# Expert layers of a macaron block: up-projection weights as the stationary operand, fed from two fixed buffers per half

## What is computed

```python
x = hidden_states.reshape(-1, H)                       # H = 256
probs = jax.nn.softmax(x @ router_w.T, axis=-1)        # 8 experts
topk_weights, selected_experts = jax.lax.top_k(probs, 2)
for e in range(E):
    ew = jnp.sum(topk_weights * (selected_experts == e), axis=-1, keepdims=True)
    h = x @ w1[e].T                                    # 256 -> 2 * 512
    gate = jax.nn.silu(h[:, :I])                       # I = 512
    y = h[:, I:] * gate @ w2[e].T                      # 512 -> 256
    out = out + y * ew
```

## Time and profile before

| | before |
|---|---|
| median of the runs | 2212.82 us |
| profiled execution, device time | 2211.96 us |
| its span, first to last instruction | 2210.2 us |
| first FFN's slots | about 131 to 552 us |
| second FFN's slots | about 1762 to 2188 us |
| TensorE busy over the span | 1602.6 us (73%) |
| VectorE, ScalarE, GpSimd busy | 1189.6, 632.5, 735.4 us |

### The profile page before, as it was taken

One profiled execution on the slowest core, in us unless ns is written; L12 is line 12 of the kernel. 1 busy time (PEld: TensorE's weight loads), 2 busy tenths in 40 slices (PEclk: granted clock), 3 DMA queues, 4 the chain that ended last, 5 costly groups with the idle time before them and its releaser, 6 DMA issues. The chain is left out here.

```text
span 2210.2 us, 62919 instructions
## 1 busy us (share of the span) xinstructions
PE 1602.6 (73%) x23284; PEld 1062.9 (48%) x23285; DVE 1189.6 (54%) x3478; ACT 632.5 (29%) x1646; POOL 735.4 (33%) x988
## 2 busy tenths in 40 slices
PE   4359999999477278572777536786357299999995
PEld 4336666666135265251643436444355156666663
DVE  7513434444256875559764696667766334344442
ACT  2111111111356234453343633446323111111110
POOL 3722222222044151550514704238044212222221
PEclk9999999999677587775887856886668599999998
DMA  9443223232101000110001000010000272323234
GB/s 293 146 160 48 45 45 45 46 45 39 52 3 28 1 19 20 41 30 0 20 20 40 10 20 15 5 58 9 3 11 29 95 233 45 48 43 48 43 48 100
DMA packets 83844, 113.32 MB, mean 51 GB/s; under 512 B 13048, under 2 KB 74944, under 8 KB 81600
## 3 DMA queue, kind: packets, MB, share of 16 engines
q1 hardware_dynamic: 57120, 75.91, 11.2%
q0 software_dynamic: 26592, 35.67, 9.7%
HBM read 63.65 MB, written 52.08 MB: 52 GB/s over the span
## 5 line engine op out<-in xcount | busy, mean ns | idle before, releaser
L591 PE MATMUL ffn_bank<-ffn_w,ffn_tileT 128*128 x1136 | 539.0, 597 | 7.4 <-DMA ffn_w<-in_w2t_dram 3.9
L712 POOL DMA_INDIRECT x<-ffn_yout,ffn_place x142 | 221.1, 1557 | 651.2 <-DVE ffn_yout L679 587.1
L650 ACT ACTIVATE ffn_gate<-ffn_bank 128x512 f32<-128x512 f32 x142 | 84.8, 597 | 706.2 <-PE ffn_bank L591 706.2
L607 PE MATMUL ffn_bank<-ffn_w,ffn_actT 128*128 x1136 | 268.6, 379 | 1.8 <-DVE ffn_actT L693 1.8
L591 PEld LDWEIGHTS ffn_bank<-ffn_w,ffn_tileT 128*128 128x128 f32 x1136 | 195.5, 192 | 148.7 <-issue 148.5
L607 PEld LDWEIGHTS ffn_bank<-ffn_w,ffn_actT 128*128 128x128 f32 x1136 | 215.7, 190 | 91.2 <-issue 69.2
L693 DVE COPY ffn_actT<-ffn_bank 128x512 f32<-128x512 f32 x142 | 98.1, 691 | 170.8 <-PE ffn_bank L599 170.8
L685 DVE TENSOR_TENSOR ffn_gate<-ffn_gate,ffn_bank 128x512 f32<-128x512 f32 x142 | 97.6, 687 | 167.1 <-PE ffn_bank L591 167.1
L1444 PE MATMUL at_bank<-pass_right,pass_left 32*32 32x48 f32 x3072 | 52.2, 231 | 83.0 <-DVE pass_right L1316 63.5
L580 PE MATMUL ffn_bank<-ffn_ident,ffn_tile 128*128 128x128 f32 x284 | 55.6, 278 | 77.5 <-DMA ffn_tile<-xs 77.3
L599 PEld LDWEIGHTS ffn_bank<-ffn_ident,ffn_gate 128*128 128x128 f32 x568 | 71.2, 141 | 73.9 <-issue 73.7
(11 more groups left out here) (493 smaller groups left out, 3252.1 us busy)
## 6 DMA issues: line engine op xcount, KB each, us to landing
ffn_tile<-xs SPq DMA_DIRECT2D x142, 130.0 KB, 2.1
ffn_w<-in_w1t_dram SPq DMA_DIRECT2D x16, 1024.0 KB, 5.2
ffn_w<-in_w2t_dram SPq DMA_DIRECT2D x16, 512.0 KB, 6.2
ffn_x<-in_x_dram SPq DMA_DIRECT2D x16, 256.0 KB, 4.8
x<-ffn_x SPq DMA_DIRECT2D x16, 256.0 KB, 6.1
pass_xa<-x SPq DMA_DIRECT2D x12, 256.0 KB, 3.6
pass_xr<-x SPq DMA_DIRECT2D x12, 256.0 KB, 2.7
x<-pass_xr SPq DMA_DIRECT2D x12, 256.0 KB, 2.1
```

The costliest lines, as they stand in the source:

```text
L591: t = pe.matmul(bank[:, :], rowsT[b][:, k * P:(k + 1) * P], w1[:, bass.ds(e * 2048 + (k * 1024 + half * INNER), INNER)], start=(k == 0), s ...
L607: t = pe.matmul(p_y[b], actT[b][:, k * P:(k + 1) * P], w2[:, bass.ds(e * 1024 + k * DIM, DIM)], start=(k == 0), stop=(k == ICH - 1))
L650: act.activation(gate[b][:, :], p_g[b][:, :], ACT.Silu).then_inc(s_silu, 1)
L712: pool.indirect_dma_start(total, bass.IndirectOffsetOnAxis(ap=place[b][:, 0:1], axis=0), yout[b][:, :], None, compute_op=ALU.add).then_inc ...
```

## The change

The stationary and the moving operand of the up-projection change places. For each slot, half and 128-column chunk of the half, a 128x128 block of `w1` is now loaded as the stationary operand and the 128 turned tokens move past. The product comes out with the inner dimension on partitions, which is the layout that `down` wants, so `turn_act` and the copy to `actT` are gone and `inner` takes the place of both `gate` and `actT`. The stationary blocks are not read at a register's address: `fetch` copies the slot's half of `w1` (128 x 1024 f32) to a fixed buffer, half 0 on ScalarE behind Silu of the slot before, half 1 on VectorE behind the product of the slot before. Each copy reads the expert's number into a register and waits for that expert's weights.

```diff
+    half_now = [[sb(f"{n}{i}", [P, KCH, INNER]) for i in range(2)] for n in ("gate_now", "up_now")]
+    def fetch(eng, copy, m, b, half):
+        e = eng.value_load(table.expert[0:1, bass.ds(m, 1)], min_val=0, max_val=EXPERTS - 1)
+        eng.wait_ge(wts.s, e * 32 + 32)
+        src = w1[:, :].rearrange("p (e k s f) -> p e k s f", e=EXPERTS, k=KCH, s=2)[:, bass.ds(e, 1), :, half, :]
+        copy(half_now[half][b][:, :, :], src.rearrange("p e k f -> p (e k) f")).then_inc(s_now[half], 1)
 # TensorE
-            def up(m, b, e, half):
+            def up(m, b, half):
+                pe.wait_ge(s_now[half], m + 1)
                 if half == 0:
-                    pe.wait_ge(wts.s, e * 32 + 32)
                     pe.wait_ge(s_xTs, m + 1)
                     if not early(m):
-                        pe.wait_ge(s_aTs, m - 1)
+                        pe.wait_ge(s_act, m - 1)
                 bank = (p_g if half == 0 else p_u)[b]
-                for k in range(KCH):
-                    t = pe.matmul(bank[:, :], rowsT[b][:, k * P:(k + 1) * P],
-                                  w1[:, bass.ds(e * 2048 + (k * 1024 + half * INNER), INNER)],
-                                  start=(k == 0), stop=(k == KCH - 1))
+                for i in range(ICH):
+                    for k in range(KCH):
+                        t = pe.matmul(bank[:, i * P:(i + 1) * P],
+                                      half_now[half][b][:, k, i * P:(i + 1) * P],
+                                      rowsT[b][:, k * P:(k + 1) * P], start=(k == 0), stop=(k == KCH - 1))
-            def turn_act(m, b):
+            def down(m, b, e):
                 pe.wait_ge(s_act, m + 1)
-                for k in range(ICH):
-                    t = pe.transpose(p_t[b][:, k * P:(k + 1) * P], gate[b][:, k * P:(k + 1) * P], ident[:, :])
-                t.then_inc(s_aT, 1)
-            def down(m, b, e):
-                pe.wait_ge(s_aTs, m + 1)
...
-                e = expert(m)
-                up(m, b, e, 0)
-                if not lead:
-                    turn_act(m - 1, 1 - b)
-                up(m, b, e, 1)
+                up(m, b, 0)
+                up(m, b, 1)
                 if not lead:
                     down(m - 1, 1 - b, expert(m - 1))
 # ScalarE
-                act.activation(gate[b][:, :], p_g[b][:, :], ACT.Silu).then_inc(s_silu, 1)
+                act.activation(inner[b][:, :], p_g[b][:, :], ACT.Silu).then_inc(s_silu, 1)
+                if not last:
+                    fetch(act, act.copy, m + 1, 1 - b, 0)
 # VectorE
-                dve.tensor_tensor(gate[b][:, :], gate[b][:, :], p_u[b][:, :], ALU.mult).then_inc(s_act, 1)
+                dve.tensor_tensor(inner[b][:, :], inner[b][:, :], p_u[b][:, :], ALU.mult).then_inc(s_act, 1)
+                if not last:
+                    fetch(dve, dve.tensor_copy, m + 1, 1 - b, 1)
                 if not (isinstance(m, int) and m == 0):
                     weigh(m - 1, j if b == 1 else j - 1, 1 - b)
                 if not last:
                     meta(m + 1, j + (b == 1), 1 - b)
-                dve.wait_ge(s_aT, m + 1)
-                if not early(m):
-                    dve.wait_ge(s_y, m - 1)
-                dve.tensor_copy(actT[b][:, :], p_t[b][:, :]).then_inc(s_aTs, 1)
```

More of the change, by code:

```diff
@@ L522, in experts @@
     rowsT = [sb(f"tileT{i}", [P, KCH * P]) for i in range(2)]
-    gate = [sb(f"gate{i}", [P, INNER]) for i in range(2)]
-    actT = [sb(f"actT{i}", [P, ICH * P]) for i in range(2)]
+    inner = [sb(f"inner{i}", [P, ICH * P]) for i in range(2)]
     yout = [sb(f"yout{i}", [P, DIM]) for i in range(2)]
@@ L529, in experts @@
     w1, w2 = wts.w1, wts.w2
+    half_now = [[sb(f"{n}{i}", [P, KCH, INNER]) for i in range(2)] for n in ("gate_now", "up_now")]
     p_x = [psum[0][:, 0:DIM], psum[1][:, 0:DIM]]
     p_g, p_u = [psum[2], psum[3]], [psum[4], psum[5]]
-    p_t = p_g
     p_y = [psum[6][:, 0:DIM], psum[7][:, 0:DIM]]
@@ L536, in experts @@
     s_g, s_u, s_silu, s_act = sem("g"), sem("u"), sem("silu"), sem("act")
-    s_aT, s_aTs, s_y, s_ys, s_go, s_id = sem("aT"), sem("aTs"), sem("y"), sem("ys"), sem("go"), sem("id")
+    s_now = [sem("gate_now"), sem("up_now")]
+    s_y, s_ys, s_go, s_id = sem("y"), sem("ys"), sem("go"), sem("id")
     def early(m):
         return isinstance(m, int) and m < 2
+    def fetch(eng, copy, m, b, half):
[3 more added lines that the diff above has]
+        copy(half_now[half][b][:, :, :], src.rearrange("p e k f -> p (e k) f")).then_inc(s_now[half], 1)
     with nc.Block() as block:
@@ L606, in down @@
                 for k in range(ICH):
-                    t = pe.matmul(p_y[b], actT[b][:, k * P:(k + 1) * P],
+                    t = pe.matmul(p_y[b], inner[b][:, k * P:(k + 1) * P],
                                   w2[:, bass.ds(e * 1024 + k * DIM, DIM)],
@@ L636, in _ @@
             step(PAIRS, 0, last=True)
-            turn_act(SLOTS - 1, 0)
             down(SLOTS - 1, 0, expert(SLOTS - 1))
@@ L641, in _, with step @@
         def _(act):
-            def step(m, b):
+            def step(m, b, last=False):
                 act.wait_ge(s_xT, m + 1)
@@ L648, in step @@
                 if not early(m):
-                    act.wait_ge(s_aT, m - 1)
-                act.activation(gate[b][:, :], p_g[b][:, :], ACT.Silu).then_inc(s_silu, 1)
+                    act.wait_ge(s_y, m - 1)
+                act.activation(inner[b][:, :], p_g[b][:, :], ACT.Silu).then_inc(s_silu, 1)
+                if not last:
+                    fetch(act, act.copy, m + 1, 1 - b, 0)
+            fetch(act, act.copy, 0, 0, 0)
             for b in range(2):
@@ L655, in _ @@
                     step(2 * j + b, b)
-            step(SLOTS - 1, 0)
+            step(SLOTS - 1, 0, last=True)
         @block.vector
@@ L689, in step @@
                     meta(m + 1, j + (b == 1), 1 - b)
-                dve.wait_ge(s_aT, m + 1)
-                if not early(m):
-                    dve.wait_ge(s_y, m - 1)
-                dve.tensor_copy(actT[b][:, :], p_t[b][:, :]).then_inc(s_aTs, 1)
+            fetch(dve, dve.tensor_copy, 0, 0, 1)
             meta(0, 0, 0)
```

## The result

The changed kernel took 2173.9 us, the median of four runs (2167.7 to 2186.2), beside 2212.2 us (2205.8 to 2214.2, four runs, one more than in the section on the kernel before): a ratio of 0.984, with a 95% interval of 0.981 to 0.987. The forecast was 2169 with a range of 2151 to 2225. The profiled execution took 2178.0 us, its span 2176.1.

What follows compares the result with a forecast made beforehand. TensorE's own work was taken to set the FFN slot: 5.83 to 5.50 us, 133 x 0.33 = 43.9 less, 1.2 more at the second FFN's start, so 42.7 off 2212.0 gives 2169.3, stated as 2169; range 2151 to 2225.

Steps and rivals of the forecast that it cites:

- The price of a pair: Up-projection on TensorE: load and 128-column matmul run side by side, 0.111 us a pair, 3.55 for 32; break-even 0.121.
- The rival in which a load shows: Up-projection: load and matmul don't hide each other wholly, 0.163 us a pair, slot 7.17, time 2390; chance 0.15.
- the 8 columns: Routing matmuls' moving columns: 0.014 us at 1.2 GHz if loads waited for matmuls; the 0.214 pace was said to exclude it.
- The slot: TensorE's steady FFN period: 0.22 turning rows, 3.55 up-projection, 1.73 down-projection, together 5.50 us, 0.33 less than 5.83.
- The start of the second FFN: A copy of 1.04 us now lies between the first weights' landing and the first matmul: some 1.2 us more.
- Late tiles as before: Some 7 slots early in the second FFN, with tiles late behind weight DMAs, were taken as unchanged.
- The copies: Weight copies of 128x1024, 1.04 us on ScalarE and 0.69 on VectorE, hidden beside TensorE's work with 0.7 to spare.
- the tile ring: VectorE's copy, `weigh`, `meta`, SyncE's load, DMA: hidden by 0.7 us, 0.15 with longer copy; late-tile rival 2205, chance 0.12.
- TensorE needs the copied half itself only after the next half 0, at 7.3.: Deadline of VectorE's copy of half 1's weights, counted in us from the start of half 0 of slot m.
- Registers on TensorE: One of two register reads per slot goes, costing nothing while TensorE's queue is full; up to 0.74 us gained behind late tiles.
- The scatter as the bound: Rival: VectorE's copy and GpSimd's descriptor work block each other, scatter's ring 5.80 us, no gain, 2209; chance 0.04.
- the change doesn't do what it says: Rival: half 0 finds its block missing, ScalarE 1.0 us later than counted; time stays at 2212; chance 0.04.

Runs made afterwards that it cites:

- half-column run: The changed kernel with only 64 of the 128 tokens moving in the up-projection (slots 0 and 1 keep all): 2177.6 us, ratio 0.984.
- the late copy: The changed kernel with VectorE's weight copy moved behind the next slot's metadata, slot 0's behind slot 0's metadata: 2306.3 us, ratio 1.043.

## Why the prediction was right, step by step

- *What bounds it.* Right: TensorE at 100% of the first FFN's stretch and over 99% of the second's at clock 1.00, before and after.
- *The price of a pair.* Right, and the main risk: 0.1116 against 0.111. The rival in which a load shows (0.121 or more) is out. By the ratio of the Trainium skill, "TensorE: Matmul & The Clock Gate", section "Back-to-back issue gap", the estimate was 0.156, and the chain's 0.1116 does not bear it out. One leg of the working could not stand by itself: the 0.214 at half clock was held against "twice 0.107", and 0.107 was itself half of 0.214, so it could not rule out that the 8 columns stand on top. The half-column run rules it out.
- *The slot.* 5.52 against 5.50, from 5.82 instead of 5.83, so 0.30 saved where 0.33 was forecast: 133 x 0.30 = 39.9, less 1.2 at the second FFN's start, is 38.7. The two FFNs gained 38.4: 20.6 for 69 x 0.30 = 20.7, and 17.8 for 64 x 0.30 - 1.2 = 18.0. Of the 4.9 us between 2169 and 2173.9 some 4.0 are this one term (133 x 0.03). The runs themselves spread from 2167.7 to 2186.2, so that the total came out so near is in part luck. (The prediction's sum also drops the 0.8 that it names: 2169.3 + 0.8 is 2170.)
- *The start of the second FFN.* Mis-sized: 1.2 forecast, 2.1 measured up to the end of slot 0's up-projection. Between the landing of the first weights and the first matmul lay 0.14 us and now lie 1.58 (1750.97 to 1752.55), since on ScalarE the copy of the turned tokens stands behind that of the weights:

```profile
1751.08 1.04 ACT L548 COPY ffn_gate_now<-ffn_w 128x1024 f32 x1 [44.34 <-DMA ffn_w<-in_w2t_dram]
1752.04 0.36 ACT L644 COPY ffn_tileT<-ffn_bank 128x256 f32<-128x256 f32 x1
```

  The other 0.6 is the up-projection itself (5.66 us to the next turned rows against 5.04 before); its first half ran at a granted clock of 0.50, while the whole of it had 0.70 before. The late tiles gave about half a us back, see next: the agreement of 17.8 with 18.0 is partly two small misses that cancel.
- *Late tiles as before.* Nearly right: the nine slots behind slot 0's up-projection took 56.6 us before and take 55.5, where the forecast allows 0.6 less. The weights of the second expert do come 2.2 us later, which the prediction did not see; sending them at the old distance left 0.6 us in the second FFN, so most of the stretch is held by later loads.
- *The copies.* Right on duration and that they hide, shown by leaving them out, by adding them to the kernel before and by multiplying them. The slack was mis-sized: 1.4 on ScalarE and 1.2 on the tile ring where both were put at 0.7, mainly since the 0.75 of the register read was counted in series and only 0.18 and 0.39 of it show behind Silu and the product. It erred to the safe side.
- *"TensorE needs the copied half itself only after the next half 0, at 7.3."* Wrong by a slot, shown by the late copy: the need is at 1.78 after the half 0 of the same slot. In the change as made the copy ends at 407.85, and half 1 of that slot starts 1.78 after 407.77, at 409.55: 1.7 of slack. The error cost the forecast nothing, since the tile ring is tighter, but it made the expectation for the late copy useless.
- *Registers on TensorE.* "Both cost nothing" holds at 5.82. In a slot of 5.38 the read costs 0.15 on the mean (5.53 - 5.38), and in this change the one ahead of half 0 is gone. Whether it would have shown at 5.52 no run tests. Behind a late tile the 0.74 is gained, as forecast: no issue time stands behind the turned rows at 1802.46.
- *The scatter as the bound* and *the change doesn't do what it says*: not seen; TensorE never waits for either in the steady slot.

## What to carry to other kernels

Before you swap stationary and moving operand, compare two paces from the trace, that of a stream of loads and that of the columns. Here 128 f32 columns under one load took as long as the load, so the swap cost almost nothing (0.13 us a slot), and going down to 64 columns brought nothing. When you ask whether moved work is hidden, write down for which slot its result is, and count to that slot's use: a copy for the next slot has a deadline inside that slot. A price that was hidden (a register read) can come out once the work over it is removed; here it came out in every second slot, so look at single slots and not only at the mean.

## What the hardware showed that was not expected

- An f32 pair of 128x128 stationary and 128 moving columns takes 0.1116 us in a stream at clock 1.00, and with 64 columns 0.111.
- A register read on ScalarE shows as 0.18 us behind a Silu of 0.60; on VectorE it shows as 0.39 behind a product of 0.69 and 0.70 behind an operation of 0.22. So part of it runs beside the operation ahead of it.
- The same attention code took 1197 to 1216 us from one profiled execution to the next, in all kernels, which is more than what separates several kernels here. TensorE and its clock vary with it: 742 us busy at a granted clock of 0.70 in the longest (1216), 710 at 0.74 in the shortest (1197), while VectorE is busy for 786 us in both. Why the clock differs was not tested.
